# Local attention's probabilities: scaling moved from GpSimd to VectorE

## What is computed

```python
x = conv_block(x)     # group norm, global attention over the 1024 pixels, projection, residual
t = to_tokens(x)      # 1024 tokens x 128
t = t + attn_block(layernorm(t))
t = t + fp8_linear(layernorm(t))
```

```python
scores = jnp.einsum('bnqhd,bnkhd->bnhqk', q, k) / np.sqrt(HD)
probs = jax.nn.softmax(scores, axis=-1)
attn = jnp.einsum('bnhqk,bnkhd->bnqhd', probs, v)
```

## Time and profile before

| what | value |
|---|---|
| median of 3 runs | 2314.04 us (2309.74 to 2316.64) |
| the profiled execution's own time | 2316.24 us |
| its span, first to last instruction | 2314.5 us |
| PE busy | 2141.3 us (93%) |
| DVE busy | 1698.6 us (73%) |
| ACT busy | 1736.7 us (75%) |
| POOL busy | 1272.5 us (55%) |
| L428, POOL's multiply | 128 x 1047 ns = 134.0 us |
| L817, DVE's transpose | 128 x 706 ns = 90.4 us |

### The profile page before, as it was taken

One profiled execution on the slowest core, in us unless ns is written; L12 is line 12 of the kernel. 1 busy time (PEld: TensorE's weight loads), 2 busy tenths in 40 slices (PEclk: granted clock), 3 DMA queues, 4 the chain that ended last, 5 costly groups with the idle time before them and its releaser, 6 DMA issues. The chain is left out here.

```text
span 2314.5 us, 59631 instructions
## 1 busy us (share of the span) xinstructions
PE 2141.3 (93%) x21394; PEld 1563.5 (68%) x21394; DVE 1698.6 (73%) x5284; ACT 1736.7 (75%) x3393; POOL 1272.5 (55%) x1576
## 2 busy tenths in 40 slices
PE   4899999999999999999999999999999999999984
PEld 2667666677766677766677766677766667766663
DVE  6677777777787777777777777777787777787753
ACT  2678777878777878777877777878777878777863
POOL 5256555566555566555556555556555556555554
PEclk8999999999999999999999999999999999999997
DMA  1111111111111111111111111111111111111110
GB/s 45 23 43 32 38 44 46 29 42 29 39 43 46 30 42 29 39 43 46 31 42 29 39 42 46 31 42 32 37 42 46 33 40 33 36 41 46 35 31 19
DMA packets 76188, 86.84 MB, mean 38 GB/s; under 512 B 20624, under 2 KB 55440, under 8 KB 76048
## 3 DMA queue, kind: packets, MB, share of 16 engines
q1 hardware_dynamic: 62368, 52.44, 9.4%
q10 hardware_dynamic: 13680, 33.04, 4.3%
HBM read 18.29 MB, written 16.78 MB: 15 GB/s over the span
## 5 line engine op out<-in xcount | busy, mean ns | idle before, releaser
L993 PEld LDWEIGHTS ps<-vg,p 128*128 128x128 f32 x4096 | 511.5, 192 | 51.9 <-issue 12.9
L993 PE MATMUL ps<-vg,p 128*128 128x129 f32 x4096 | 537.9, 278 | 0.7 <-ACT p L544 0.7
L392 POOL TENSOR_SCALAR nmean<-mv 128x4 f32<-128x4 f32 x256 | 58.3, 228 | 575.3 <-DVE mv L763 572.0
L544 ACT ACTIVATE p<-ps 128x512 f32<-128x512 f32 x512 | 300.2, 587 | 91.1 <-PE ps L887 90.6
L725 DVE TENSOR_REDUCE cm<-ps 128x1 f32<-128x512 f32 x512 | 334.0, 679 | 15.5 <-PE ps L949 13.9
L537 ACT ACTIVATE ps<-shift 128x512 f32<-128x512 f32 x512 | 300.9, 596 | 17.4 <-ACT p L544 0.7
L428 POOL TENSOR_TENSOR e<-e,srec 128x512 f32<-128x512 f32 x128 | 134.0, 1047 | 241.5 <-DVE srec L808 241.5
L394 POOL TENSOR_TENSOR rstd<-veps,halfpow 128x4 f32<-128x4 f32 x256 | 265.8, 1038 | 0.0
L1089 PE MATMUL ps<-w,hid 128*128 128x128 f32 x2048 | 242.2, 277 | 5.2 <-ACT hid L596 2.0
L1089 PEld LDWEIGHTS ps<-w,hid 128*128 128x128 f32 x2048 | 233.5, 192 | 8.6 <-ACT hid L596 8.6
L587 ACT ACTIVATE oh<-ps 128x512 f16<-128x512 f32 x64 | 38.2, 597 | 240.2 <-PE ps L1057 240.2
(11 more groups left out here) (180 smaller groups left out, 5501.3 us busy)
## 6 DMA issues: line engine op xcount, KB each, us to landing
ptbd<-et SPq DMA_DIRECT2D x512, 64.0 KB, 2.0
kbd<-kk SPq DMA_DIRECT2D x512, 32.0 KB, 2.0
out_y<-o_sb ACTq DMA_DIRECT2D x64, 256.0 KB, 2.0
x_sb<-in_x ACTq DMA_DIRECT2D x31, 512.0 KB, 4.0
x_sb<-in_x SPq DMA_DIRECT2D x1, 512.0 KB, 3.5
e<-in_w_t SPq DMA_DIRECT2D x1, 256.0 KB, 3.6
w<-in_w_t SPq DMA_DIRECT2D x1, 256.0 KB, 3.6
hid<-in_in_w_t SPq DMA_DIRECT2D x1, 192.0 KB, 2.5
```

The lines of the kernel that those rows point to most:

```text
L544: sc.activation(p32[:, c % PRING, :], bank("st", c), ACT.Exp, scale=C ** -0.5).then_inc(s["p_made"], 1)
L993: last = mm(ps[:, b, at:at + PVW], p32[:, c % PRING, part], vg32[:, j, :], start=j == 0 and q % 2 == 0, stop=j == MT - 1, skip_group_check ...
```

## The change

GpSimd's step `prob` and its four entries in GpSimd's list are taken out. The same multiplication is put on VectorE, at the head of `turn_p`, right before the transpose. The semaphores stay: the multiplication waits for `srec_made` and signals `prob_made`, and the transpose waits for `prob_made`, now both on VectorE. VectorE's list is unchanged, and so is everything else.

```diff
     "pool": """
-        prob1:0-- bias_out:1-- keep:0-- out:0-- prob0:1-- prob1:1-- norm_mid:0-- keep:1-- down:0-- out:1--
+        bias_out:1-- keep:0-- out:0-- norm_mid:0-- keep:1-- down:0-- out:1--
         norm_out:0-- norm_mid:1-- ln_q:0-- ln_in:0- quant:0-- down:1-- bias_out:0- norm_out:1-- ln_q:1-- gn2:0
-        quant:1-- prob0:0- ln_in:1-""",
+        quant:1-- ln_in:1-""",
...
-            def prob(pair):
-                def step(kind, img, h):
-                    n = 2 * img + h
-                    pool.wait_ge(s["srec_made"], upto(n, pair + 1, per=2))
-                    g.tensor_tensor(by_head(e[:, h, pair, :]), by_head(e[:, h, pair, :]), spread(srec[:, h, pair, :]),
-                                    ALU.mult).then_inc(s["prob_made"], 1)
-                return step
...
             def turn_p(pair):
                 def step(kind, img, h):
+                    dve.wait_ge(s["srec_made"], upto(2 * img + h, pair + 1, per=2))
+                    v_.tensor_tensor(by_head(e[:, h, pair, :]), by_head(e[:, h, pair, :]), spread(srec[:, h, pair, :]),
+                                     ALU.mult).then_inc(s["prob_made"], 1)
                     dve.wait_ge(s["prob_made"], upto(2 * img + h, pair + 1, per=2))
```

More of the change, by code:

```diff
@@ L454, in norm_out @@
                 g.tensor_tensor(u[:, h], u[:, h], w[:, h], ALU.add).then_inc(s["t2_made"], 1)
-            run(pool, "pool", {"gn2": gn2, "ln_in": power_step(0), "out": power_step(1), "bias_out": bias_out, "norm_mid": norm_mid, "keep": keep, "prob0": prob(0), "prob1": prob(1), "quant": quant, "down": power_step(2), "norm_out": norm_out,
+            run(pool, "pool", {"gn2": gn2, "ln_in": power_step(0), "out": power_step(1), "bias_out": bias_out, "norm_mid": norm_mid, "keep": keep, "quant": quant, "down": power_step(2), "norm_out": norm_out,
                        "ln_q": power_step(3)}, prologue)
```

## The result

The changed kernel takes 2374.11 us (median of 3 runs, 2372.03 to 2381.09) against 2314.04 us: 1.0273 times as long, 95% interval 1.0253 to 1.0292, or 60 us more. It was forecast slower, at 2401 us with a range of 2350 to 2420. The direction and both places of the loss were right; both prices were too high.

A forecast was written before the change was run, and what follows sets the result against it. VectorE was taken as the bound in each image's stretch ahead of `cmax`. 1.4 us there plus 1.4 us ahead of `pv1:1` made 2.8 us per image, 87 us over 31 images: 2401 us, range 2350 to 2420.

The forecast's parts named there:

- both places of the loss: Per image, ahead of `cmax` in h=0 and ahead of `pv1:1` in h=1, 1.4 us each.
- The bound and the place of the first cost: h=0 ahead of `cmax`: VectorE is the bound there, and two multiplies of 0.73 us come in.
- the slack of 0.22: h=0, ahead of `max:1`: 0.22 us absorbed from the multiplies' 1.46, leaving 1.24 us.
- The additions that took it to 1.4: h=0, over 1.24 us: late `place1:0` transfers delaying `max:7` up to 0.2, and `nshift` meeting the first multiply, 0 to 0.2.
- Rival (b): h=0: second multiply collides with GpSimd's `bias_out:1`, VectorE waits 1.0 to 1.2 more; 2435 us; chance 0.08.
- The collision in h=1: First h=1 multiply, ready 0.18 us inside GpSimd's `keep:1`, waits for its end, 1.1 us.
- one row of another form: Setup: a 128x128 VectorE product by a column took 11.68 us, until GpSimd's last memset ended; cited for the wait.
- Its price: h=1: copies issued late make `pv1:1` start 1.2 to 1.7 us later with the wait, taken as 1.4.
- Held multiply: Sign in the changed profile: one multiply in four held while `keep:1` runs, as a long record or a gap.
- TensorE's wait at the turned shift grown: Sign in h=0: this wait grows along with a `qg:0` to `cmax` distance longer by 1.2 to 1.5 us.
- `pv1:1` waiting 1.5 to 2 us: Sign in h=1: TensorE waits this long ahead of `pv1:1` instead of 0.36 us.
- Rival (a): h=1: the multiply runs freely beside GpSimd; 1.7 us per image, 2367 us; chance 0.33.

The follow-up runs named there:

- e4: e3 with a GpSimd memset of 128 x 960 f32 put behind `norm_mid:0`, where `keep:1` was: 2364.52 us, ratio 1.0224.
- e3: The changed kernel with GpSimd's `keep:1` moved ahead of `out:0`: 2365.48 us, ratio 1.0219.
- e6: The kernel before, with the next image's input load issued behind ScalarE's `pv1:1` instead of in front of it: 2295.79 us, ratio 0.9926.
- e2: The kernel before with only the two h=0 multiplies moved to VectorE, those of h=1 left on GpSimd: 2350.49 us, ratio 1.0154.
- e10: The kernel before with only the h=1 multiplies on VectorE, `keep:1` ahead of `out:0`, the input load behind `pv1:1`: 2297.26 us, ratio 0.9947.

## Why the prediction came out as it did

**The bound and the place of the first cost: right.** VectorE's full stretch ahead of `cmax` took both multiplies at their price. The duration was right (0.68 against 0.69 from the earlier trace rows), and so were the dependent transpose (0.72 and 0.71 against 0.73) and the slack of 0.22. The sum was 1.24; 1.07 came out. The missing 0.17 is a few hundredths each: the two price terms, and `max:0`, `qg:1` and `turn_in:1`, which now start 0.17, 0.55 and 0.57 behind their predecessors instead of 0.20, 0.60 and 0.61. The additions that took it to 1.4 cost nothing: `nshift` was the one to be lengthened (below), and `pv1:0`'s copies didn't delay `max:7`. That is the first mis-sized term, 1.4 against 1.07, some 10 us.

**Rival (b): not there, by the margin given.** GpSimd after, in h=0:

```profile
1083.53 0.76 POOL L401 TENSOR_TENSOR nshift<-nmean,rstd 128x4 f32<-128x4 f32 x1
1087.24 1.52 POOL L412 TENSOR_TENSOR y<-y,rows 128x512 f32<-128x512 f32 x1 [2.95 <-PE ps L1000]
```

`bias_out` is 0.29 behind the multiply of 1086.95 (0.26 was worked out) and is itself stretched, from 1.26 to 1.52 us. `nshift` takes 0.76 instead of 0.20 beside the multiply of 1083.55, although it starts 0.02 ahead of it. VectorE is not delayed in either: both multiplies take 0.68.

**The collision in h=1: right in time and length.** `norm_mid:0` moved up to ScalarE's end, `keep:1` ran into the multiply 0.17 ahead of it (0.18 was worked out), and the hold was 0.97 us (1.1). That the wait was taken was in part luck. It rested on one row of another form, in which memsets hold a product that reads one tile and a column; e4 shows that a memset doesn't hold this multiply, so that row was no evidence for it. What bears it out is e3 and e4. And the sentence that no overlap of the steady stage before had two SBUF inputs on VectorE is wrong. In all images but one a small operation on `gmv` and `gtmp` ran beside GpSimd's `rstd`:

```profile
489.70 1.04 POOL L394 TENSOR_TENSOR rstd<-veps,halfpow 128x4 f32<-128x4 f32 x1
```

```profile
489.71 0.20 DVE L696 TENSOR_TENSOR gtmp<-gmv,gtmp 128x1 f32<-128x1 f32 x1
```

It took 0.20 us in the 31 overlaps and 0.16 in the one image without, far from GpSimd's 1.04. So an overlap of this kind need not cost GpSimd's whole record; no run here shows whether its 4 columns or its kind of operation makes the difference.

**Its price: the step that failed.** The prediction said that `pv1:1` starts 1.84 to 2.37 us after the last issue, and carried every delay of the issues through to TensorE: 1.2 to 1.7 us with the hold, 0.1 to 0.6 without. The 1.84 of `pv1:0` was no lower bound: in the changed kernel the issues end at 1112.75 and `pv1:1` starts 1.46 later, at 1114.21. And the 2.37 was the load's doing: the 512 KB load stands at a fixed place, and copies issued behind it land together after it, so that a later issue moves them far less than its own delay. From before to after the last issue moved by 1.5 us and the last landing by 0.60. `pv1:1` thus came 0.70 later with the hold and 0.48 without, against forecasts of 1.4 and 0.3. The load was named, for 0.1 us; that the last copies of `place0:1` would slip behind it wasn't, and this is what makes `pv0:1` wait. This is the larger of the mis-sized terms, 0.7 us per image or 22 us.

**The signs named.** Held multiply: yes, one in four. VectorE's idle ahead of the second transpose: gone. `qg:0` to `cmax` longer by 1.2 to 1.5: by 1.07. TensorE's wait at the turned shift grown: no, it is 0.57 in both kernels, since the time is lost earlier, at the row maxima (L944 behind VectorE waits 16.7 us in all and L1000 25.1; the same lines before, L949 and L1005, waited 0.8 and 1.2). `pv1:1` waiting 1.5 to 2 us: no, `pv0:1` by 1.0 in the image shown, 1.26 in the mean.

**Rival (a)** gave 2367 and came nearer to the median than the forecast, but its premise, a multiply that runs free, is false; e3, where it does run free, took 2365.48. Since the stated range took in both sums, the measured time alone says nothing on whether the multiply is held; the 1.66 us record does.

## What to carry to other kernels

Price an operation on the stretch where its new engine works back to back, not on the engine's share: two multiplies of 0.69 us cost 1.07 us per image in h=0, where VectorE had 0.22 to spare. Taking work off an engine moves what was queued behind it, and that can collide with the very work that was moved: look up what will run then, and whether both engines read SBUF. And where a transfer ends a wait, look at which other transfer is issued close to it: putting the input load 5.6 us later made the old kernel 0.7% faster, while no placing of the multiply tried here gained anything.

## What the runs showed of the hardware

A VectorE multiply with two SBUF operands took 1.66 us instead of 0.69 when GpSimd's `keep:1`, which has SBUF inputs, had started 0.17 us before it, and 0.68 beside a memset of 0.90 us. The other way round, GpSimd's `nshift` took 0.76 instead of 0.20 us, and `bias_out` 1.52 instead of 1.26. A held operation shows as a longer record, not as idle time in front of it.

A 64 KB copy landed 2.0 us after its issue when no load was under way (the copies of h=1 in e6). Where its issue ended 0.1 us after that of a 512 KB load from another queue, it took 4.6 us and landed 0.2 us behind the load (the fourth copy of h=1 in e3).

In the setup the hold of the earlier trace rows comes and goes: the product that took 11.68 us before took 0.78 in the changed kernel, whose setup is the same. VectorE after:

```profile
25.08 0.78 DVE L645 TENSOR_SCALAR res<-res,cols 128x128 f32<-128x128 f32 x1
```

Here VectorE got in between the memsets, and eight of them took 8.13 instead of 7.20 us. The product took 10.4 to 11.7 us in the profiles of before, e2, e3 and e10, and 0.3 to 1.1 in the eight others, and the first image follows: its h=0 to h=1 was 36.4 to 36.6 us in before, e2 and e3, 34.9 in e10, and 30.2 to 30.5 in the others. So some 4 to 6 us of a profiled execution hang on it, and short comparisons are better made on the period.
